# Attention and expert layer on one core: the order of VectorE's early low halves and of the normalised rows of batch 6

## The reference, cut to what matters

```python
x = _layernorm(x + attn(x))   # 16 heads of 16, RMS norm and rotation of q and k, causal softmax, projection
# ffn: normed = x * rsqrt(mean(x^2)) * norm_weight
# shared = relu(normed @ sw1 + sb1) @ sw2 + sb2
# the 2 best of 8 experts for each token, each relu(flat @ ew1 + eb1) @ ew2 + eb2, weighted and summed
x = _layernorm(x + shared + routed)
```

## Time and profile before

| | |
|---|---|
| median of 3 runs (lowest, highest) | 999.18 us (998.37, 1002.56) |
| the profiled execution's own time | 1000.01 us |
| its span, first to last instruction | 998.3 us |
| mean granted TensorE clock | 0.983 |
| TensorE / VectorE / ScalarE / GpSimd busy | 911.2 / 600.1 / 624.2 / 433.5 us |
| idle time of VectorE before the 12 early low halves (L1271), put down to "issue" | 8.3 us, 2 times |

### The profile page before, as it was taken

How to read it: one execution, slowest core, us unless ns; L and a number is a source line. 1 busy time by engine, 2 the same in 40 slices (tenths; PEclk the granted TensorE clock), 3 DMA queues, 4 the chain that set the end, 5 groups by cost and what they waited for, 6 DMA issues and landing times.

```text
span 998.3 us, 26472 instructions
## 1 busy us (share of the span) xinstructions
PE 911.2 (91%) x9048; PEld 694.1 (70%) x9049; DVE 600.1 (60%) x1185; ACT 624.2 (63%) x1023; POOL 433.5 (43%) x637
## 2 busy tenths in 40 slices
PE   4589999997988987989899999999999999999995
PEld 1244555554554644877799899899999988688884
DVE  6756799888888855666234444444443332238875
ACT  3489898887888875434446655655654554556753
POOL 4654556877767654464024233432413233212211
PEclk9899999999999999999999999999999999999998
DMA  6011323434323255376882121221212121157641
GB/s 209 22 64 64 117 96 102 133 107 150 107 86 119 97 206 206 104 278 215 280 264 94 43 75 47 70 65 52 75 44 73 49 80 56 40 153 241 203 158 43
DMA packets 69539, 116.98 MB, mean 117 GB/s; under 512 B 7792, under 2 KB 45808, under 8 KB 69328
## 3 DMA queue, kind: packets, MB, share of 16 engines
q1 hardware_dynamic: 52080, 81.51, 24.7%
q10 hardware_dynamic: 10896, 16.40, 5.6%
q0 software_dynamic: 6480, 17.97, 5.0%
HBM read 68.67 MB, written 47.18 MB: 116 GB/s over the span
## 4 chain that ended last, share of the span: by engine, by line
PE 59%; POOL 14%; DVE 9%; issue 7%; ACT 5%; DMA 4%; ACTq 0%; SPq 0%; POOLq 0%; DVEq 0%
PE hb L1705 24%; PE yb L1721 23%; DMA xg_rows<-xnh,sl_i 3%; PE pv_bank L1502 3%; POOL xg_rows L679 3%; POOL nat L641 2%; PE ma L1511 2%; ACT prob L806 2%; PE tr L1584 2%; POOL rsum L632 1%; PE slot L1480 1%; POOL nat L648 1%; POOL nat L649 1%; POOL rsum L629 1%; POOL y L688 1%
## 5 line engine op out<-in xcount | busy, mean ns | idle before, releaser
L960 ACT ACTIVATE hf<-hb,b 128x256 f32<-128x256 f32 (+1 forms) x392 | 154.7, 456 | 228.0 <-PE hb L1705 224.2
L1705 PE MATMUL hb<-xgT,wts 128*128 128x256 f16 (+1 forms) x1872 | 219.8, 264 | 2.6 <-ACT hf L960 2.1
L1361 DVE TENSOR_TENSOR hh<-hf,hh 128x1024 f16<-128x1024 f32 (+1 forms) x98 | 118.7, 1211 | 168.6 <-ACT hh L965 130.4
L1721 PE MATMUL yb<-wts,hh 128*128 x1704 | 215.3, 273 | 0.1
L1705 PEld LDWEIGHTS hb<-xgT,wts 128*128 x1872 | 178.3, 98 | 25.3 <-issue 3.9
L734 POOL DMA_INDIRECT y_tok<-yb,dest x71 | 73.6, 1037 | 272.7 <-DVE yb L1373 255.2
L1721 PEld LDWEIGHTS yb<-wts,hh 128*128 128x128 f16 x1704 | 166.5, 98 | 21.8 <-issue 0.6
L806 ACT ACTIVATE prob<-slot 128x1024 f32<-128x1024 f32 x160 | 162.2, 1043 | 30.2 <-PE slot L1489 29.0
L965 ACT ACTIVATE hh<-hf 128x1024 f16<-128x1024 f32 (+1 forms) x98 | 97.6, 996 | 3.1
L1511 PE MATMUL ma<-wqkv,xTh 128*128 128x512 f16 (+1 forms) x384 | 79.7, 356 | 17.4 <-DVE xTh L1030 10.3
L1480 PE MATMUL slot<-stk 64*128 64x128 f16 (+3 forms) x512 | 63.5, 306 | 19.3 <-ACT prob L806 9.4
(11 more groups left out here) (197 smaller groups left out, 1422.6 us busy)
## 6 DMA issues: line engine op xcount, KB each, us to landing
wts<-in_w_all SPq DMA_DIRECT2D x19, 512.0 KB
stage<-in_w_all SPq DMA_DIRECT2D x16, 512.0 KB
w_split<-chunk_hl SPq DMA_DIRECT2D x16, 512.0 KB
wts<-y_tok SPq DMA_DIRECT2D x32, 256.0 KB, 4.6
xg<-xg_rows ACTq DMA_DIRECT2D x30, 264.0 KB
wts<-w_split SPq DMA_DIRECT2D x3, 2048.0 KB
xTf<-in_xT SPq DMA_DIRECT2D x8, 512.0 KB, 3.6
xin<-in_x SPq DMA_DIRECT2D x8, 512.0 KB, 4.3
```

The source lines that it names most:

```text
L960: act.activation(hf[:, c, 0:size], hb[c // 2][:, (c % 2) * TT:(c % 2) * TT + size], ACT.Relu, bias=bias, scale=1.0 / WS).then_inc(S("relu_ ...
L1361: dve.tensor_tensor(hh[:, par, 1, cs, 0:size], hf[:, cs, 0:size], hh[:, par, 0, cs, 0:size], ALU.subtract).then_inc(S("h_lo"), 1)
L1705: ins = pe.matmul(hb[hc // 2][:, (hc % 2) * TT:(hc % 2) * TT + size], weights(e, c, w, hc * P, P), xgT[:, par, x * DC + c, 0:size], start= ...
L1721: ins = pe.matmul(ybank[par][:, j * D:(j + 1) * D], hh[:, par, x, hc, P * j:P * j + P], weights(e, DC + hc * D // CH, w, hc * D % CH, D), ...
```

## The change

Two things are changed. VectorE's low half of an early piece H(m,q) is issued at p+3 and not at p+2, and within the step it comes behind the division and split of attended tiles, the projection's addition and the normalised rows, and ahead of `chosen`, `weighed` and `ranked`. The rows of batch 6 are made at 157 and 161 and not at 158 and 163.

```diff
 def rows_due(g):
-    return due(XN_ROWS, g) if g < NPOS * (NB - 1) + XN_ROWS_LAST[0] else [
-        (NB - 1, u) for u, off in enumerate(XN_ROWS_LAST) if NPOS * (NB - 1) + off == g]
-
-
-assert NPOS * (NB - 2) + max(XN_ROWS) < NPOS * (NB - 1) + XN_ROWS_LAST[0]
+    return [(c, u) for c in range(NB) for u, off in enumerate(XN_ROWS if c < NB - 2 else XN_ROWS_LAST) if NPOS * c + off == g]
@@ step of VectorE
                     for kind, m, q in early_due(g - 2):
-                        if kind == "H":
-                            early_low(m, q)
-                        elif q == 1:
+                        if kind == "O" and q == 1:
                             if m == N_EARLY - 1:
                                 turned(0, 0)
                                 turned(0, 1)
@@
                     for c, u in rows_due(g):
                         normalised(c, u)
+                    for kind, m, q in early_due(g - 3):
+                        if kind == "H":
+                            early_low(m, q)
                     for c, _ in due(LG, g):
                         chosen(c)
```

## The result

| | before | after |
|---|---|---|
| median of 18 runs each (lowest, highest) | 998.21 us (991.44, 1002.56) | 990.64 us (983.43, 994.23) |
| span of the profiled execution | 998.3 us | 987.9 us |
| mean granted TensorE clock | 0.983 | 0.986 |

The ratio is 0.9924, with a 95% interval of 0.9909 to 0.9939: the changed kernel is 7.6 us faster (6.1 to 9.1). The prediction was 991.8 us, 7.4 us less than before.

A forecast was written before the change was run, and what follows sets the result against it. TensorE was taken to bound (busy 91%), stalled 4.75 us by VectorE's order. Waits 5.6, clock 1.4 and tails 0.5 make 7.5, taken as 7.4: profiled 1000.01 to 992.6, median 991.8 us; own range 989.5 to 994, chance 0.70.

The forecast's parts named there:

- The place and the mechanism: VectorE: nat(7,0), holding bank `mb`, stands behind low(0,0), which waits for ScalarE's high half; moved ahead, TensorE's 4.75 us wait goes.
- The sum: PROJ(7,0) on TensorE starts at 406.95 in place of 414.36, 7.4 us earlier; the term lies between 4.5 and 7.5.
- list of starts: TensorE's pieces from NAT(7,1) at 393.39 to PROJ(7,0) at 406.95, with no wait: 13.56 us at full speed.
- The part for the clock: TensorE's slow clock behind the 4.75 us wait, 0.50 and then 0.77 up to 403.00: 1.4 us to be regained.
- rows(6,0) ahead of added(6,1): VectorE: added(6,1) starts 0.56 us late; GpSimd's shifted rows taken 0.6 late, at 390.2, other end 389.6.
- low(2,0) and low(2,1): VectorE: 1.2 us gained behind added(7,1) and 1.2 us paid behind rows(7,1) cancel; value 0, ends -2 and +2.
- The cast of rows(6,1) beside a scatter instruction: VectorE at about 391: GpSimd could hold this cast, using up the 0.9 us margin ahead of NAT(7,1).
- a shrinking shift: Sign of being wrong: the shift, about 7.4 us at every later landmark if right, shrinks between PROJ(7,0) and L1584.
- A: Wait only moved to nat(7,1) and nat(7,2): 2 us of waits and 1.4 of clock remain, gain 4, 995.2; chance 0.13.
- B: Gain given back before the routed tiles, scatter landings setting GpSimd's roots of (7,0): gain 2 to 3, about 997; chance 0.08.
- C: Slower: many short pauses up to PROJ(7,0), clock staying at 0.50, 6.1 us more than before, 1005.3; chance 0.04.
- D: No effect: VectorE idle until 394.20 again, say because GpSimd's rows of (6,1) are late, 999.2; chance 0.05.

The follow-up runs named there:

- low(0,0) alone: Kernel before with only low(0,0) moved, behind rows(6,1) and nat(7,0), everything else as before; ratio to before 0.9927 (0.9905 to 0.9950).
- low halves alone: Kernel before with only the low halves moved as in the change, rows of batch 6 staying at 158 and 163; ratio to before 0.9904 (0.9874 to 0.9934).
- rows alone: Kernel before with only the rows of batch 6 moved (157 and 161), low halves as before; run twice, ratios to before 0.9952 and 0.9979.
- H(4,0) at 196: Changed kernel with TensorE's H(4,0) at 196, not 197, between RANK(7) and the count of the tables; ratio to before 0.9929 (0.9899 to 0.9960).

## Why the prediction was right

**The place and the mechanism** are as predicted: nat(7,0) stood behind a low half that waited for ScalarE. low(0,0) alone removes the 4.75 us; rows ahead of it without low(0,0) moved shorten the wait by their 2.1 us and no more.

**The sum**, 7.4 us at PROJ(7,0), measured 7.44 to 7.49 between all pairs of profiles. (That the timed gain, 7.6 us, is as near to it is in part luck: its interval is 6.1 to 9.1, and the landmarks further on shift by less, see below.) Its list of starts, one after the other at full speed, was 13.56 us from NAT(7,1) on, and is 405.11 - 391.62 = 13.49. The part for the clock (1.4 us) was paid back in full.

**rows(6,0) ahead of added(6,1)**, taken at 0.6 us late on GpSimd: the margin at NAT(7,1) came out at 1.3 us and not 0.9. The shifting of (6,1) took GpSimd 387.77 - 384.04 = 3.73 us from the first root, against 389.60 - 385.28 = 4.3 before, when VectorE's rows ran beside it. So nearly nothing was given on, the other end of the range.

**low(2,0) and low(2,1)** cancel, value 0: from AT(7,1) to LG(7) the kernels with and without these moves agree within 0.04 us.

**What the prediction missed.** It looked at the contention between VectorE and GpSimd only for casts, in two places, and both readings came out otherwise. The cast of rows(6,1) beside a scatter instruction was not held (0.43 us). At GpSimd's first residual addition it had nat(7,3); the cast of split(7,1) stood there and took 1.51 us, as 1.49 in the low halves alone, where nothing was lost by it. GpSimd's timeline after:

```profile
388.10 1.31 POOL L675 DMA_INDIRECT xg_rows<-xnh,sl_i  x1 [0.29 <-POOL xnh L673]
...
399.54 1.28 POOL L705 TENSOR_TENSOR rs<-rs,b2s 128x512 f32<-128x512 f32 x1
...
405.34 1.27 POOL L705 TENSOR_TENSOR rs<-rs,b2s 128x512 f32<-128x512 f32 x1
```

What cost time was the second residual addition, beside `chosen(6)`: in two of the three profiles it held an instruction with two inputs, in the third a cast of 8 elements. The Trainium skill (SBUF — State Buffer, Who interferes with whom) also names VectorE's instructions with two inputs in SBUF, against a GpSimd instruction that reads SBUF; 1.99 us for L1162 and 2.47 for a low half beside L705 agree with it. The trace of the kernel before had such a row too, the subtraction of rows(7,1), 2.35 us for 0.69:

```profile
432.44 2.35 DVE L1147 TENSOR_TENSOR xnh<-xnf,xnh 128x512 f16<-128x512 f32 x1
...
432.95 1.28 POOL L709 TENSOR_TENSOR rs<-rs,b2s 128x512 f32<-128x512 f32 x1
```

The second residual addition came 15.05 us behind H(0,1) before and 16.34 now, while `chosen(6)` came some 7 us earlier, and so the two meet. GpSimd had 2.5 us of room before the roots of (7,0), as predicted (3 us), yet it delayed VectorE. That costs 0.6 to 1.0 us: the shift at AT(7,1) is 6.4 to 6.9 us in the three profiles of the changed kernel, and 7.5 in the one with the low halves alone, where the two didn't meet.

**Behind PROJ(7,0)** the prediction had every landmark shifted alike, and named a shrinking shift as a sign of being wrong. It does shrink: from 7.5 us at PROJ(7,0) to between 6.4 and 6.9 at AT(7,1). It stays there up to LG(7), and is 6.3 to 7.0 at the first turn of gathered rows. The routed part starts 4.6 to 8.5 us earlier, by pair of profiles; the mean of two before (87.0) less the mean of three after (80.6) is 6.4 us. The landing of the gathered rows and the clock behind the waits for them vary from execution to execution by more than the rest. Timed, 7.6 us (6.1 to 9.1) and 7.1 (4.9 to 9.3) hold both 6.4 and 7.4.

**The rivals.** A, the wait moved: not in the whole change; low(0,0) alone shows new waits of 2.06 and 0.94 us, but without the slow clock that A had behind them. B, the landings of scatters hold the roots of (7,0) back: no, GpSimd waited 2.54 us for VectorE's statistics there; what the shift lost behind PROJ(7,0) is the contention. C, a clock that stays low: 1.00 throughout the stretch. D, VectorE idle as before: no, rows(6,1) start at 387.34 and low(0,0) at 392.36.

## What to carry to other kernels

On an in-order queue, look for the instruction that waits longest and ask whether what stands behind it is ready and wanted; then follow all the later waits of the same queue before moving one, because low(0,0) alone gave 4.1 of 7.5 us. A wait that is only shortened can give almost nothing: of 2.1 us, 1.15 went to a later wait on the same queue, where an instruction now met GpSimd's, and 0.31 to the clock. Compare kernels by a stretch between two landmarks: up to PROJ(7,0) it repeated to 0.1 us where whole executions scatter by some 10 us. But choose it short: up to the routed part the same kernel varied by 3 us, and the price at AT(7,1) shows only beyond PROJ(7,0).

## What the runs showed that was not expected

A wait of 2.65 us was followed by a slower H(1,0) (4.28 and 4.29 us in the two profiles of rows alone) than the wait of 4.75 us (3.55); the transposes ahead of it were slow only behind the long one (0.89 against 0.47 us). Behind 2.06 us in the kernel with low(0,0) alone nothing was slow (clock 1.00). The length of the wait doesn't decide it: ahead of AT(7,1) the third profile of the changed kernel waited 1.91 us and went on at full speed, the one with H(4,0) at 196 waited 1.92 us and took 4.29 us for H(2,0) in place of 2.62.

An addition of 32 elements per partition went from 0.19 to 1.99 us beside a GpSimd addition of 1.27 us, though its record starts 0.66 us ahead of that addition's. In these runs what was added went by the other instruction and not by one's own length: 1.80 us for this one, 1.23 for a cast of 8 elements, 1.08 to 1.42 for casts of 512, 1.66 for a subtraction of 512, 1.16 to 1.40 for low halves of 1024, all beside GpSimd additions of 1.27 or 1.28 us.

A part of the scatter of the runs arises early: from the first PROJ of the span to PROJ(6,1) the profiles took 267.55 to 268.21 us (113.85 to 381.72 in the kernel before, 108.64 to 376.21 in the earliest), while that first PROJ started anywhere from 108.64 to 113.85. What varies there was not tried.
